# Macaron block (experts, attention, experts) on one core: the experts' sums weighted on VectorE in one step and added to the stream by GpSimd

## What is computed

```
x = x + 0.5 * ffn(layernorm(x));  x = x + attn(layernorm(x));  x = x + 0.5 * ffn(layernorm(x))

ffn:  gate = x @ Wg.T + bias; the 4 greatest of 8 experts; softmax over them -> weights
      out = swiglu(x, Ws1, Ws2, Ws3)                               # the shared expert
      out = out + sum over e of weights[:, e] * swiglu(x, W1[e], W2[e], W3[e])
attn: 16 heads of 64, causal mask, softmax, output projection 1024 -> 128
```

## Time and profile before

| | us |
|---|---|
| median of 3 runs | 685.54 |
| range of the runs | 685.2 to 688.0 |
| span of the profiled execution, first to last instruction | 683.0 |

### The profile page before, as it was taken

How to read it: one execution, slowest core, us unless ns; L and a number is a source line. 1 busy time by engine, 2 the same in 40 slices (tenths; PEclk the granted TensorE clock), 3 DMA queues, 4 the chain that set the end, 5 groups by cost and what they waited for, 6 DMA issues and landing times.

```text
span 683.0 us, 20985 instructions
## 1 busy us (share of the span) xinstructions
PE 646.1 (95%) x7846; PEld 414.1 (61%) x7846; DVE 609.6 (89%) x1701; ACT 572.8 (84%) x1110; POOL 495.7 (73%) x589
## 2 busy tenths in 40 slices
PE   5798989999999998999899999999999999999997
PEld 3465755465567565666566566665666567666665
DVE  4899799999998999899889999989999888789887
ACT  6789977898999888899978999997999997565654
POOL 3244775688899687788967889895789898566555
PEclk9999999999999999999999999999999999999999
DMA  7800000278799366588844788683678797100000
GB/s 205 258 1 1 1 2 1 54 111 148 120 129 154 57 104 120 100 140 123 145 75 79 114 140 141 125 137 56 102 125 134 144 144 110 33 1 18 17 2 16
DMA packets 226489, 62.97 MB, mean 92 GB/s; under 512 B 213202, under 2 KB 225620, under 8 KB 226388
## 3 DMA queue, kind: packets, MB, share of 16 engines
q1 hardware_dynamic: 226388, 61.64, 52.4%
HBM read 7.87 MB, written 1.05 MB: 13 GB/s over the span
## 4 chain that ended last, share of the span: by engine, by line
PE 45%; DVE 23%; ACT 16%; issue 9%; POOL 5%; DMA 1%; SPq 0%; ACTq 0%; DVEq 0%; POOLq 0%
PE bank L1068 13%; PE bank L1070 12%; PE bank L1069 12%; ACT probs L1424 6%; DVE probs L1710 4%; DVE glu L1619 3%; DVE xs L1649 3%; ACT glu L1386 3%; PE bank L1238 3%; DVE glu L1624 3%; POOL paired L1035 2%; ACT gluh L1407 2%; PE bank L1201 2%; POOL glul L1031 1%; ACT paired L1432 1%
## 5 line engine op out<-in xcount | busy, mean ns | idle before, releaser
L1031 POOL TENSOR_TENSOR glul<-glu,gluh 128x512 f16<-128x512 f32 x191 | 221.3, 1161 | 98.4 <-ACT gluh L1407 97.9
L1035 POOL TENSOR_TENSOR paired<-probs,paired 128x512 f16<-128x512 f32 x160 | 185.4, 1161 | 27.4 <-ACT paired L1432 24.5
L1386 ACT ACTIVATE glu<-bank,tanh_scale 128x512 f32<-128x512 f32 x167 | 113.3, 678 | 49.1 <-PE bank L1070 48.5
L1619 DVE SCALAR_TENSOR_TENSOR glu<-glu,bank 128x512 f32<-128x512 f32 x167 | 113.7, 681 | 24.8 <-ACT glu L1386 24.4
L1424 ACT ACTIVATE probs<-probs,exp_bias 128x128 f32<-128x128 f32 (+3 forms) x256 | 131.6, 551 | 3.6 <-POOL exp_bias L1043 3.5
L1710 DVE CUSTOM_DVE_ANT_0 probs<-bank,causal,score_scale 128x128 f32<-128x128 f32 (+3 forms) x256 | 128.0, 545 | 6.2 <-POOL paired L1035 5.0
L1068 PE MATMUL bank<-w3h,gluh 128*128 128x128 f16 x708 | 127.4, 220 | 5.9 <-POOL glul L1031 4.9
L1070 PE MATMUL bank<-w3h,glul 128*128 128x128 f16 x708 | 127.2, 220 | 0.0
L1069 PE MATMUL bank<-w3l,gluh 128*128 128x128 f16 x708 | 127.2, 220 | 0.0
L1407 ACT ACTIVATE gluh<-glu 128x512 f16<-128x512 f32 x191 | 118.5, 621 | 2.0 <-DVE glu L1624 2.0
L1624 DVE SCALAR_TENSOR_TENSOR glu<-glu,bank 128x512 f32<-128x512 f32 x167 | 114.7, 687 | 5.8
(11 more groups left out here) (236 smaller groups left out, 1619.8 us busy)
## 6 DMA issues: line engine op xcount, KB each, us to landing
pT<-paired SPq DMA_TRANSPOSE x160, 3.2
attention_raw<-in_L_attn_W_qkv SPq DMA_DIRECT2D x6, 256.0 KB, 5.3
xs<-in_L_attn_inputs SPq DMA_DIRECT2D x4, 256.0 KB, 4.7
vh<-in_L_ffn_W SPq DMA_DIRECT2D x6, 128.0 KB
pT<-in_L_ffn_W SPq DMA_DIRECT2D x6, 128.0 KB
out<-xs SPq DMA_DIRECT2D x3, 256.0 KB, 2.5
raw_more<-in_L_ffn_W SPq DMA_DIRECT2D x4, 128.0 KB
attention_raw<-in_L_attn_W_out SPq DMA_DIRECT2D x2, 256.0 KB, 6.4
```

What stands on the lines that cost most here:

```text
L1031: pool.tensor_tensor(glul[pair][:, :], g[:, :], gluh[pair][:, :], ALU.subtract).then_inc(glu_low)
L1035: pool.tensor_tensor(paired[n % PAIRED][:, 1, :], probs[n % PROBS][:, :], paired[n % PAIRED][:, 0, :], ALU.subtract).then_inc(probs_low)
L1386: act.activation(g[:, :], psum[b1.bank][:, :], ACT.Tanh, scale=tanh_scale[:, j:j + 1]).then_inc(tanh_made)
L1619: v.scalar_tensor_tensor(g[:, :], g[:, :], 1.0, psum[b1.bank][:, :], ALU.add, ALU.mult).then_inc(drained[b1.bank])
```

## The change

For experts 1 to 7 of every layer, collect is replaced by two steps. DVE multiplies the whole bank (512 columns) by the weights in one `tensor_tensor`, the weights being read with a stride of zero over the 128 columns of each group, into one of three new buffers `product`; this frees the bank. POOL then adds the product to the stream with one `tensor_tensor` of 512 columns, at the end of the same step (`add_experts`), behind that step's `glul`. The order of the stream is kept: a new semaphore `added` counts POOL's sums, the next reader of the stream waits for it (`Added`), and DVE waits with a fourth product until the first one has been added. Expert 8 is collected by DVE as before, in four instructions, after POOL's last sum. The shared expert (n = 0), whose scale is the same for all rows, is added by DVE in one instruction of 512 columns instead of four.

```diff
         def collect(i):
             while collects and collects[0][0] < i:
                 _, n, use, done = collects.pop(0)
-                self.add("collect", c=c, b=b, n=n, use=use, done=done, stream=self.stream_at[b])
                 self.release(use)
                 self.route_left[c % 2] = use
+                if 0 < n < NE - 1:
+                    self.add("weigh_expert", c=c, n=n, use=use, done=done, m=self.products)
+                    owed.append((self.products, use))
+                    self.products += 1
+                    continue
+                add_experts()
+                self.add("collect", c=c, b=b, n=n, use=use, done=done, stream=self.stream_at[b])
                 self.stream_at[b] = use
...
             for j, n in parts:
                 self.down(c, j, n, tiles, done)
             collects += [(i + COLLECT_LAG - 1, *of) for of in done]
+            add_experts()
...
+                elif kind == "add_expert":
+                    b, m, use, stream = s["b"], s["m"], s["use"], s["stream"]
+                    if isinstance(stream, Added):
+                        q.wait_ge(added, stream.n)
+                    else:
+                        q.wait_ge(drained[stream.bank], stream.n + stream.d)
+                    q.wait_ge(drained[use.bank], use.n + use.d)
+                    pool.tensor_tensor(stream_of(b), stream_of(b), product[m % PRODUCTS][:, :], ALU.add).then_inc(added)
...
+                elif kind == "weigh_expert":
+                    c, n, use, m = s["c"], s["n"], s["use"], s["m"]
+                    route_there(c, n)
+                    if m >= PRODUCTS:
+                        q.wait_ge(added, m - PRODUCTS + 1)
+                    q.wait_ge(down_done, s["done"])
+                    by_rows = lambda ap: ap[:, :].rearrange("p (t d) -> p t d", d=D)
+                    v.tensor_tensor(by_rows(product[m % PRODUCTS]), by_rows(psum[use.bank]),
+                                    route[c % 2][:, n, :].unsqueeze(2).broadcast_to([P, NT, D]), ALU.mult
+                                    ).then_inc(drained[use.bank])
                 elif kind == "collect":
                     c, b, n, use = s["c"], s["b"], s["n"], s["use"]
                     stream_ready(b, s["stream"])
+                    if n == 0:
+                        q.wait_ge(down_done, s["done"])
+                        v.scalar_tensor_tensor(stream_of(b), psum[use.bank][:, :], unscale[:, 0:1], stream_of(b),
+                                               ALU.mult, ALU.add).then_inc(drained[use.bank])
+                        continue
```

More of the change, by code:

```diff
@@ L126 @@
 VALUES_AT = [3, 8, 13, 18]
+PRODUCTS = 3
 BANKS = 8
@@ L139 @@
 Turned = namedtuple("Turned", "n")
+Added = namedtuple("Added", "n")
 class Schedule:
@@ L149, in __init__ @@
         self.drains, self.fills = [0] * BANKS, [0] * BANKS
-        self.splits = self.norms = self.turned_norms = self.tiles = self.parts = 0
+        self.splits = self.norms = self.turned_norms = self.tiles = self.parts = self.products = 0
         self.glu_taken = 0
@@ L392, in feed_forward, with add_experts @@
     def feed_forward(self, c, b, halves, prepare):
-        tiles, collects, later = {}, [], []
+        tiles, collects, later, owed = {}, [], [], []
         order = TILE_ORDER if c else range(HT)
         late = {}
+        def add_experts():
+            for m, use in owed:
+                self.add("add_expert", b=b, m=m, use=use, stream=self.stream_at[b])
+                self.stream_at[b] = Added(m + 1)
+            owed.clear()
         def collect(i):
@@ L775, in macaron @@
         attn = [sb(f"attn{i}", [P, NT, P]) for i in range(2)]
+        product = [sb(f"product{i}", [P, L]) for i in range(PRODUCTS)]
         attn_pair = [sb(f"attn_pair{i}", [P, 2, NT * P], F16) for i in range(2)]
@@ L796, in macaron @@
         rows_made = signal("rows_made")
+        added = signal("added")
         consts_made = signal("consts_made")
@@ L1461, in low_of, with route_there @@
                 made.then_inc(drained[split.use.bank] if part is None else part)
+            def route_there(c, n):
+                weights = route[c % 2][:, n, :]
+                q.wait_ge(route_made, c + 1)
+                if c == 0:
+                    chained(v.tensor_scalar(weights, weights, unscale[:, n:n + 1], None, ALU.mult))
+                    chain()
             def stream_ready(b, use):
@@ L1465, in stream_ready @@
                     q.wait_ge(x_in[b], 16)
+                elif isinstance(use, Added):
+                    q.wait_ge(added, use.n)
                 else:
@@ L1649, in vector @@
                         done = v.scalar_tensor_tensor(rows, psum[use.bank][:, t * D:(t + 1) * D],
-                                                      route[c % 2][:, n, t:t + 1] if n else unscale[:, 0:1], rows,
-                                                      ALU.mult, ALU.add)
-                        if c == 2 * B - 1 and n == NE - 1 and t % 2:
+                                                      route[c % 2][:, n, t:t + 1], rows, ALU.mult, ALU.add)
+                        if c == 2 * B - 1 and t % 2:
                             done.then_inc(rows_made)
-                    if c < 2 * B - 1 or n < NE - 1:
+                    if c < 2 * B - 1:
                         done.then_inc(drained[use.bank])
```

## The result

The changed kernel takes 698.05 us (median of 4 runs, 697.37 to 699.89) beside 686.64 us for the kernel before (4 runs again, 685.2 to 688.0): a ratio of 1.0171, with a 95% interval of 1.0147 to 1.0196. It is slower by 1.7%, some 12 us, where 1 us less was forecast and 690.5 us was the end of the range. The profiled execution has a span of 698.2 us, 15.2 us more than that of before. By the medians the difference is 11.4 us.

What follows compares the result with a forecast made beforehand. PE, 95% busy, was taken as the bound. Gains of 5.0 us, POOL's cost of 2.7 and the tail's 1.3 gave -1.0 on a 683.0 us span; with 2.5 from span to median, 684.5 us, range 678.5 to 690.5.

Steps and rivals of the forecast that it cites:

- What VectorE gains: DVE's collects: multiply 0.685 us, 0.44 us saved per weighted expert, 27.6 us less load with the shared expert.
- the 5.0 us of gain: PE's idle beside attention: ten waits for collects shrink by 4.4 us, waits for other DVE instructions by 0.6.
- The price of an addition: POOL's addition of 512 columns, priced from L1031: 1.12 us each, bounds 1.0 to 1.35, 63 us for 56.
- What POOL pays: Beside attention: POOL's 34 us on the chain times 0.070 additions per us, 2.4 additions, costing 2.7 us.
- The tail: After PE's last matmul: the last collect waits for two POOL additions and starts 1.3 us later (1.1 to 1.8).
- The idle that was to hide them: Beside attention: POOL's 82 us idle there could cover additions, the lower bound of their cost being 0.
- Rival 1: POOL sets the pace in three full stretches beside attention: seven additions cost 7.8 us, time 689.6 us; chance 0.20.
- its signs: Signs of POOL's queue setting the pace: L1710's waits for paired far above 5 us, POOL's chain share above 10%.
- point of decision: In POOL's full stretches: its queue sets the pace once its backlog exceeds the four probs buffers.
- Rival 3: POOL's additions hold up DVE's router ranking (L1584): 0.86 us in seven routers, 6.0 us, time 690.5 us; chance 0.04.

Runs made afterwards that it cites:

- the dose runs: Changed kernel with POOL's addition on 4 columns, on 256, on all 512, or with a second equal-sized instruction in front: 681.1, 686.4, 698.05, 732.6 us.
- the runs by layer: Changed kernel with products and additions only in layers 0, 6, 7 (688.69 us, ratio 1.0029), or only in layers 1 to 5 (697.88 us, ratio 1.0144).

## Why the prediction was wrong

- **What VectorE gains: right.** The multiply takes 0.683 us (forecast 0.685); a zero stride costs nothing. DVE's busy time is 592.6, not 582; with additions of 4 columns it is 583.8, so most of the rest is held time of steps like L1589, 668 ns on average from 218. Of the 5.0 us of gain the kernel with 4-column additions shows 4 us by its ratio and 5.6 by the medians, with its own small POOL time still in it.
- **The price of an addition: 1.12 taken, 1.28 measured** (in a full queue the next instruction starts 1.23 us after it). It lay within the bounds (1.0 to 1.35). I took L1031 for the nearest row although one of its inputs is float16. The run with float16 products shows that this matters little for the end.
- **What POOL pays: this is the step that failed.** I put 2.7 us for it. The runs with 4 columns and with 512 differ by 16.9 us; less the tail's 1.6, it is 15.3. With the gain of 5.6 us and the tail's 1.6 that makes 11.3 us, where 11.4 were measured, all by medians; by the ratios it is 14.2 us, with a gain of 4.0. The form of the estimate was wrong: POOL's share of the chain of before (5%, 34 us) times the density of additions tells what the additions cost that happen to fall on a chain that exists. It leaves out the chains that the additions make. The share rose to 16% (112 us of 698), and the dose runs show a slope rising from 0.18 to 0.38 to 0.59, where the forecast's 2.7 us for 63 are 0.04.
- **The idle that was to hide them.** I counted POOL's idle 82 us beside attention as cover. Over the kernel POOL had 187 us idle (683.0 - 495.7) and has 135 (698.2 - 562.9): of 67 us more work, 52 went into idle time, and the span, with the gain and the clock in it, grew by the other 15. Before, most of that idle was waiting for ACT's high halves (97.9 us for glul, 24.5 for paired) and these are now 63.9 and 12.4. My reading: an idle time that ends with an input's arrival covers work only if that work is over by then; an addition that starts late in the gap delays the next low half, and what is behind it.
- **Rival 1 named the mechanism, too cheaply.** Its sign and its engine were right, its signs came as written (the wait of L1755, which was L1710, at 17.6 us, POOL's share of the chain above 10%). Its price counted seven additions in three full stretches, at 1.12 us. The loss comes in steps all over 120 to 580 us. And its point of decision, the four probs buffers, carries only some 2 us of it.
- **Rival 3: half right.** DVE is held more than before, but mostly not where I looked. Of the ranking's steps L1584, now L1620, takes 0.694 us on average instead of 0.748, and two others with two SBUF inputs take a little more (L1622 0.436 instead of 0.302, L1626 0.509 instead of 0.421), while L1589, a 128x4 step with one SBUF input, wasn't on my list: 0.17 us at best, 2.65 at worst (0.53 before). Whether it reaches the end no run shows: the move of L1589 to POOL, which was to tell, leaves its work behind the same run of POOL. The Trainium skill ("GPSIMD Engine Reference", section 8, Key points) names instructions in a two-port mode beside those with two SBUF inputs; L1589, with a single tensor input and a long hold, would be one of the first kind; no run shows the mode that it ran in.
- **The tail: right.** 1.3 us forecast, 1.57 in the profile, and gone from the profile of the run without it.
- **What stays open.** Of the 15 us through POOL, late buffers carry some 2; for late low halves at PE the runs show no part that can be measured. What is left, held steps on DVE, late biases (ACT waits 10.2 us for them, 3.5 before) and the latency of norm, router and softmax loops through POOL, was not taken apart. The run with two more small POOL steps in the norm, 5 us of work for 6 us of time, points at such loops and doesn't prove them. Where PE loses the time can be read from the twins of its matmuls in the kernels with 4 and with 512 columns: behind 45 us the lag grows by 16.1 us, 6.5 of it at the scores (`kh,qh`), 6.2 at the down products (`w3h,gluh`, behind glul) and 1.7 at the heads' products (`vh,pT`, behind paired). At the scores PE waits for the low halves of q and k, which DVE makes. In the changed kernel, then in the kernel before:

```profile
PE bank L1265 <- DVE kl L1487: 3.7, 5, 1.2
PE bank L1265 <- DVE ql L1487: 2.9, 3, 1.6
...
PE bank L1238 <- DVE kl L1460: 1.0, 1, 1.0
...
PE bank L1238 <- DVE ql L1460: 0.4, 1, 0.4
```

  These 6.6 us instead of 1.4 are waits for DVE by name, but DVE has less to do than before. It stands itself for POOL (17.6 us), and the q and k come out of the norm, whose small steps and low half are POOL's. The scores are the largest place of the loss, and no run was made for them. A step of the lag says where a delay is seen, not that slack given there would win it back: with down one step later PE no longer stood for glul, and the distance stayed.

## What to carry to other kernels

An engine's idle time isn't free room: ask for each gap what ends it, and price a new instruction by the work that it stands in front of, not by the engine's average load. An engine at 82% can be dearer to load than a busier one: going from 82 to 89% beside attention cost most of 15 us, where the relief of the second-busiest gave 4 to 5.6. Where an added cost is uncertain, measure two or three doses: the slope at the first says nothing about the slope at the full one.

## What the runs showed of the hardware

- GpSimd's `tensor_tensor` over 128x512 into float32: 1.276 us with two float32 inputs, 1.160 with one float32 and one float16, 1.040 with one float32 tensor given twice. 256 columns take 0.730, 4 columns 0.199 us.
- A VectorE instruction that reads and writes SBUF alone can stand until GpSimd's run of back-to-back instructions ends: 0.17 us of work took 2.02 us and once 2.65, which is longer than two of GpSimd's instructions (1.16 us); 512 columns took 0.684 to 1.718 us. Not every such instruction is held: beside the same GpSimd the norm's statistics on xs took 0.274 to 0.294 us in all 48 cases, and the reduction over 128x256 (L1629) 0.420 or 0.421 in all 8. With one input in PSUM all 56 multiplies of 512 columns took 0.676 to 0.692 us beside the same GpSimd.
- The lower clock comes in some executions and not in others, at the same place of the program. PE pauses behind the first router in both kernels, 2.4 us in the changed one and 2.8 before. In the changed one it then ran at the lower of its two clocks from 92.3 to 95.7 us, which cost it 1.4 us; in the profiled execution of before, with the longer pause, it didn't. The stretch 90 to 100 us of the changed kernel (the clock is the third number from the end; 0.83 is the mean over the stretch, where a part is at 1.2 GHz and the rest at 2.4):

```profile
90.00:100.00 10.00, 8.24 (x58) 4.80 (x59) 7.13 (x14) 6.08 (x12) 9.02 (x10) 0.83 0.00 0
```

  And of the kernel before:

```profile
90.00:100.00 10.00, 8.90 (x76) 5.36 (x77) 8.84 (x20) 7.39 (x13) 9.16 (x9) 1.00 0.00 0
```

  Executions of one kernel differ by such stretches, about 1 to 2.5 us in all (the 21 runs of before that were measured with the runs by layer lie at 684.9 to 688.3 us, with mean clocks from 0.995 down to 0.990). So effects below 0.2% can't be told here.
